# A state-space and expert layer split into two sequence halves that share one loop

## What is computed

```python
xn = layernorm(x)                                  # (4, 512, 128)
# branch 1: a diagonal state-space scan, 16 states per channel
dt = softplus(xn @ W_dt.T + b_dt)
state[n] = exp(-dt * exp(A_log[:, n])) * state[n] + dt * B[:, n] * xn      # along the sequence
y = sum_n state[n] * C[:, n] + D * xn
# branch 2: 64 experts (128 -> 32 -> 128), top 8 of a softmax router, and 2 shared experts (128 -> 256 -> 128)
cw = normalised top-8 of softmax(xn @ router_w + router_b)                 # (tokens, 64)
routed = sum_e cw[:, e] * (silu(xn @ W1[e] + b1[e]) @ W2[e] + b2[e])
shared = sum_s silu(xn @ SW1[s] + sb1[s]) @ SW2[s] + sb2[s]
x = x + y + routed + shared
```

## Time and profile before

| what | us |
|---|---|
| median of 3 runs | 466.41 (465.42 to 468.53) |
| span of the profiled execution | 473.9 |
| TensorE busy | 346.5 |
| VectorE busy | 347.8 |
| ScalarE busy | 261.5 |
| GpSimd busy | 243.2 |

### The profile page before, as it was taken

The page is one execution under the profiler, slowest core; times in us unless marked ns, Lnnn a source line. Parts: engine busy times, 40 slices in busy tenths (PEclk is TensorE's granted clock), DMA queues, the critical chain, the costliest instruction groups (busy, mean ns, idle before and its releaser), DMA issues.

```text
span 473.9 us, 5780 instructions
## 1 busy us (share of the span) xinstructions
PE 346.5 (73%) x1491; PEld 247.2 (52%) x1491; DVE 347.8 (73%) x615; ACT 261.5 (55%) x440; POOL 243.2 (51%) x254
## 2 busy tenths in 40 slices
PE   1846879667975987779506848977887887887883
PEld 0435659356854866668403524544554554554542
DVE  5679998897864866648169759908688688688674
ACT  1477654546458346374505675355856856856820
POOL 3475300704763676776800049005577877877850
PEclk9977675959997898998956975997999999999997
DMA  6374100100111112120160000004658658668574
GB/s 175 94 200 128 25 1 1 45 11 24 46 39 29 34 41 81 43 42 21 35 190 0 0 0 2 0 0 89 126 101 161 123 116 163 122 119 162 112 152 111
DMA packets 36213, 35.09 MB, mean 74 GB/s; under 512 B 12166, under 2 KB 30839, under 8 KB 36183
## 3 DMA queue, kind: packets, MB, share of 16 engines
q0 software_dynamic: 7104, 21.90, 22.7%
q1 hardware_dynamic: 29078, 12.84, 10.2%
HBM read 13.29 MB, written 4.65 MB: 38 GB/s over the span
## 4 chain that ended last, share of the span: by engine, by line
PE 35%; POOL 19%; DVE 19%; issue 13%; ACT 6%; DMA 3%; another core or an unknown queue 2%; DVEq 1%; SPq 0%; POOLq 0%; ACTq 0%
POOL state L568 10%; PE psum L1376 5%; POOL xn_tok L572 4%; PE psum L1349 4%; POOL g_hi L581 3%; PE psum L1365 3%; PE psum L1389 3%; PE psum L1443 3%; PE psum L292 3%; PE psum L293 2%; PE psum L294 2%; PE psum L1352 2%; PE psum L1355 2%; PE psum L1338 1%
## 5 line engine op out<-in xcount | busy, mean ns | idle before, releaser
L1212 DVE TENSOR_TENSOR_SCAN state<-dec,win_t 128x1024 f32<-128x1024 f32 x32 | 73.4, 2293 | 26.5 <-ACT dec L777 26.5
L568 POOL TENSOR_SCALAR state<-state,ssm_cb 128x1024 f32<-128x1024 f32 x32 | 49.7, 1553 | 48.0 <-DVE state L1212 45.0
L812 ACT ACTIVATE sil<-psum,vec_t 128x512 f32<-128x512 f32 x64 | 43.2, 687 | 48.3 <-PE psum L294 37.7
L509 POOL DMA_INDIRECT parts<-t_out,part x39 | 41.0, 1050 | 48.3 <-ACT t_out L726 41.9
L1498 PE MATMUL psum<-hid,g_w 128*128 128x512 f32 x128 | 62.1, 599 | 0.0
L1221 DVE TENSOR_TENSOR hid<-sil,psum 128x512 f32<-128x512 f32 x64 | 41.7, 676 | 12.9 <-ACT sil L812 10.9
L497 POOL DMA_INDIRECT x_tile<-normed,token x39 | 41.3, 1059 | 13.4 <-issue 10.7
L292 PE MATMUL psum<-xn_hi,g_hi 128*128 128x512 f32 x64 | 39.7, 620 | 11.3 <-ACT sil L812 11.3
L1094 DVE TENSOR_TENSOR t_hid<-t_sil,psum 128x352 f32<-128x352 f32 x39 | 20.3, 521 | 32.3 <-ACT t_sil L710 23.5
L717 ACT ACTIVATE t_hid_t<-psum 128x384 f32<-128x384 f32 x39 | 19.2, 492 | 38.9 <-PE psum L1365 25.3
L1376 PE MATMUL psum<-w_out,t_hid_t 128*128 x234 | 37.5, 300 | 2.2 <-ACT t_out L726 1.4
(11 more groups left out here) (308 smaller groups left out, 887.6 us busy)
## 6 DMA issues: line engine op xcount, KB each, us to landing
xn_tok<-state POOLq DMA_DIRECT2D x32, 512.0 KB, 4.5
e_raw<-in_L_ffn_w SPq DMA_DIRECT2D x16, 128.0 KB, 2.2
both<-parts SPq DMA_DIRECT2D x4, 512.0 KB, 5.6
e_raw<-in_L_ffn_w SPq DMA_DIRECT2D x8, 176.0 KB, 2.6
res<-in_L_attn_x SPq DMA_DIRECT2D x4, 256.0 KB, 3.8
normed<-rows SPq DMA_DIRECT2D x1, 1024.0 KB, 5.2
g_raw<-in_L_ffn_w SPq DMA_DIRECT2D x16, 64.0 KB, 2.3
g_w<-in_L_ffn_w SPq DMA_DIRECT2D x16, 64.0 KB, 2.2
```

Source lines behind the costliest of these rows:

```text
L509: pool.indirect_dma_start(out=parts, out_offset=bass.IndirectOffsetOnAxis(ap=part[:, n:n + 1], axis=0), in_=t_out[n % ORING][:, :], in_off ...
L568: own(pool.tensor_scalar(state[k][:, :], state[k][:, :], ssm_cb[:, i * GPI + k // 2:i * GPI + k // 2 + 1], 0.0, ALU.mult, ALU.add))
L812: act.activation(sil[:, c % 2, :], ps[c % 2][:, :], ACT.Silu, bias=vec_t[:, V_B1 + c // NBLK:V_B1 + c // NBLK + 1]).then_inc(h_silu, 1)
L1212: dve.tensor_tensor_scan(state[k][:, :], dec[n % DECS][:, at_half], win_t[:, at_half], 0.0, ALU.mult, ALU.add).then_inc(scanned, 1)
```

## The change

The four blocks become two parts: blocks 0 and 1, then blocks 2 and 3. Each part is scanned and run through all 16 groups in 4 turns (4 groups by 2 blocks, and 4 states, in each), so there are 8 turns with 8 units and 4 scans each, as before. The first part's head runs alone; the second part's head (logits, `W_dt` products, shared experts, ranking, softplus, token weights) is spread over the first part's turns, and the first part's tail over turns 4 and 5. All expert weights are loaded at once (four DMAs for `g_raw1`, ahead of the shared weights in SyncE's queue, one for `g_w2` behind `both`), and GpSimd splits them in one piece before the loop. The selectors are float32r, in two tensors. Decays and scans are of one state and one half of the tokens, with 6 decay buffers. There are 4 silu buffers and 8 gated ones. Each selector product stands one unit later, behind the next unit's first product, and second products follow six products behind. The accumulating DMAs alternate between `y_t` and a second sum `y_2`, which is added at the end. GpSimd normalises the eight late tiles. The scans no longer alternate with pairs of gatings: two come first in a turn, one after two gatings, one at the end.

The core of the diff:

```diff
+        DECS, HRING = 6, 8
+        dec = [later(f"dec_{j}", [P, NTOK // 2]) for j in range(DECS)]
+        SRING = 4
+        LAG = 6
+        UNITS_BESIDE = {(0, 0, 2): [("logit", 0, 2), ("logit", 0, 3)], (0, 0, 4): [("delta", 0, 2)],
+                        (0, 0, 5): [("delta", 0, 3)], (0, 1, 2): [("shared", 0, 2), ("shared", 1, 2)],
+                        (0, 2, 2): [("shared", 2, 2), ("shared", 3, 2)],
+                        (0, 3, 3): [("shared", 0, 3), ("shared", 1, 3)],
+                        (0, 3, 5): [("shared", 2, 3), ("shared", 3, 3)]}
@@ SyncE
             sp.wait_ge(fr_dve, max(FR_DVE.values()))
+            for n in range(4):
+                at_e = slice(n * E1 // 4, (n + 1) * E1 // 4)
+                sp.dma_start(g_raw1[:, at_e, :], rw1[at_e, :, :].rearrange("e d h -> d e h")).then_inc(g_in, 16)
             sp.dma_start(sw1_raw[:, :, :], sw1.rearrange("e d h -> d e h")).then_inc(late_in, 16)
@@ GpSimd
+            pool.wait_ge(g_in, 16 * 4)
+            pool.wait_ge(both_used, 1)
+            split(raw, g_hi[:, :, :].rearrange("p g h -> p (g h)"), g_lo[:, :, :].rearrange("p g h -> p (g h)"))
+            pool.nop().then_inc(g_split, 1)
+            pool.wait_ge(late_root, 1)
+            for t in range(HT, NT):
+                pool.tensor_scalar(xn_tok[:, t, :], res[:, t, :], mv[:, t, 0:1], nrm[:, 2, t:t + 1],
+                                   ALU.subtract, ALU.mult).then_inc(late_tok, 1)
...
+            def add_state(m):
+                pool.wait_ge(scanned, m + 1)
+                own(pool.tensor_scalar(state[k][:, :], state[k][:, :], ssm_cb[:, n:n + 1], 0.0, ALU.mult, ALU.add))
+                if n >= 2:
+                    pool.wait_ge(y_in[(m - 2) % 4], 16 * ((m - 2) // 4 + 1))
+                y = (y_t, y_2)[n % 2]
+                pool.dma_start(y[:, h * HTOK:(h + 1) * HTOK], state[k][:, :], accum_op=ALU.add).then_inc(y_in[k], 16)
...
+            for m in range(2 * NS):
+                add_state(m)
+                if m in range(GPT, GPT + 3):
+                    poly_step(POOL_POLY[1], m - GPT)
+                if m == 13:
+                    skip_term(1)
@@ ScalarE, after the first part's head
+            for h, i in TURN_LIST:
+                for s in range(GSTEPS):
+                    for what in units_at(h, i, s):
+                        leave(what)
...
+                if (h, i) == (0, 0):
+                    softplus_exp(2)
+                    softplus_exp(3)
+                if (h, i) == (0, 1):
+                    choice_exp(1)
+                if (h, i) == (0, TURNS - 1):
+                    act.wait_ge(win_ready, NBLK)
+                    for m in states_of(1, 0):
+                        decay(m)
+                elif i < TURNS - 1:
+                    for m in states_of(h, i + 1):
+                        decay(m)
+                if (h, i) == (0, 1):
+                    softplus_log(2)
+                    softplus_log(3)
@@ VectorE, the head's end and the loop
+            join(0)
+            join(1)
+            variance(0)
+            reverse_root(0)
+            for t in range(HT):
+                normalise(t)
+            join(2)
+            low_part(0)
+            low_part(1)
+            join(3)
+            variance(1)
+            reverse_root(1)
+            dve.nop().then_inc(late_root, 1)
+            rank(0)
+            combine(0)
+            poly(0)
+            split_cw(0)
+            split_cw(1)
+            softplus(0)
+            softplus(1)
+            low_part(2)
+            low_part(3)
+            for h, i in TURN_LIST:
+                m = h * NS + i * GPT
+                scan(m)
+                scan(m + 1)
+                if (h, i) == (0, 1):
+                    rank(1)
+                if (h, i) == (0, 2):
+                    combine(1)
+                    poly(2)
+                if (h, i) == (0, 3):
+                    split_cw(2)
+                    softplus(2)
+                for s in range(GSTEPS):
+                    if s == 2:
+                        scan(m + 2)
+                    if (h, i, s) == (0, 3, 3):
+                        split_cw(3)
+                    if (h, i, s) == (1, 1, 4):
+                        finish(0)
+                        finish(1)
+                    weigh(h, i, s)
+                if (h, i) == (0, 3):
+                    softplus(3)
+                scan(m + 3)
+                if (h, i) == (1, 0):
+                    sum_up(0)
+                    sum_up(1)
@@ TensorE
+            def select(e):
+                pe.wait_ge(cw_split, b + 1)
+                if e >= 2:
+                    pe.wait_ge(hid_done, e - 1)
+                pe.matmul(ps[2 + e % 2][:, :], selector, blk(cw_hl, b), start=True, stop=True).then_inc(cwx_made, 1)
...
+                    for what in units_at(h, i, s):
+                        enter(what)
+                        if what[0] == "expert":
+                            selects(NTH_EXPERT[what])
+                        if what[0] in ("shared", "expert"):
+                            second_products(NTH_PRODUCT[what] - LAG + 1)
+                last = units_at(h, i, GSTEPS - 1)[-1]
+                if at_turn + 1 < len(TURN_LIST):
+                    ahead = [units_at(*TURN_LIST[at_turn + 1], s)[-1] for s in range(2)]
+                    enter(ahead[0])
+                    selects(NTH_EXPERT[ahead[0]])
+                    enter(ahead[1])
+                    selects(NTH_EXPERT[ahead[1]])
+                selects(NTH_EXPERT[last] + 1)
+                second_products(NTH_PRODUCT[last] + 1)
+                if at_turn + 1 < len(TURN_LIST):
+                    selects(NTH_EXPERT[last] + 3)
```

More of the change, by code:

```diff
@@ L184, in program @@
         tile_e = sb("tile_e", [1, NTILE], mybir.dt.int32)
+        routed = over(base, nc.sbuf_base)
+        prob, rest1 = (routed(n, [P, NT // 2, E1]) for n in ("prob", "rest1"))
         base = here()
@@ L590, in _ @@
+            for c in range(3):
+                poly_step(POOL_POLY[0], c)
+            skip_term(0)
+            for m in range(2 * NS):
[4 more added lines that the diff above has]
+                    skip_term(1)
         @block.scalar
@@ L807, in silu @@
[L807 to L824 removed]
+                act.wait_ge(g_split, 1)
@@ new lines, in _ @@
+            act.activation(warm[:, 0:1], half_pi[:, :], ACT.Sqrt)
+            root(0)
+            leave(("turn", 0, 0))
+            leave(("turn", 0, 1))
+            leave(("logit", 0, 0))
+            leave(("logit", 0, 1))
+            root(1)
+            leave(("delta", 0, 0))
+            leave(("delta", 0, 1))
+            choice_exp(0)
+            for b in range(HB):
+                softplus_exp(b)
+            for b in range(HB):
+                softplus_log(b)
+            leave(("shared", 0, 0))
@@ L1108, in _, with tiles_of, join @@
             dve.wait_ge(back_dve, max(BK_DVE.values()))
-            for b in range(NBLK):
+            def tiles_of(h):
+                return slice(h * HT, (h + 1) * HT)
+            def join(b):
                 dve.wait_ge(both_in[b], 16)
@@ L1245, in _ @@
+            for b in range(HB, NBLK):
+                sum_up(b)
+            for b in range(HB, NBLK):
+                finish(b)
         @block.tensor
@@ L1409, in _, with bank_of, turn_in_tokens @@
                     attention(b)
-            turn_tiles(xn_tok, 0, 2 * NT)
             pe.wait_ge(weights_split, 2)
             pe.wait_ge(late_in, 16 * 8)
-            for b in range(NBLK):
+            pe.wait_ge(sel_ready, 1)
+            def bank_of(what):
+                u = NTH[what]
+                if u >= 2:
+                    pe.wait_ge(h_left, u - 1)
+                return ps[u % 2]
+            def turn_in_tokens(b):
+                bank = bank_of(("turn", 0, b))
+                for n in range(TPB):
+                    if b < HB:
+                        pe.wait_ge(tok_ready, 2 * NT + b * TPB + n + 1)
+                    else:
+                        pe.wait_ge(late_tok, (b - HB) * TPB + n + 1)
+                    ins = pe.transpose(bank[:, n * P:(n + 1) * P], xn_tok[:, b * TPB + n, :], ident[:, :])
+                ins.then_inc(h_made, 1)
@@ L1456, in second_biases, with enter @@
+            def enter(what):
+                kind, k, b = what
+                if kind == "logit":
+                    logit(b)
+                if kind == "delta":
+                    delta(b)
+                if kind == "shared":
+                    shared_in(k, b)
+                if kind == "expert":
+                    expert_in(k, b)
             def second_biases(b):
                 pe.wait_ge(cw_copied, b + 1)
-                pe.matmul(ps[4 + b][:, :], b2_sb[:, :], cw_b2[:, b % 2, :], start=False, stop=False,
+                if b == NBLK - 1:
+                    pe.wait_ge(cw_split, NBLK)
+                pe.matmul(ps[4 + b][:, :], b2_sb[:, :], cw_b2[:, b % 2, :], start=b == NBLK - 1, stop=False,
@@ L1515, in _, with second_product @@
```

(15 more changed lines are left out.)

623 lines of the change are left out of this document (305 added, 318 removed).

## The result

The changed kernel takes 473.78 us (median of 4 runs, 472.45 to 474.68) against 466.72 (median of 4, 465.42 to 468.53) in the same job: ratio 1.0143, 95% interval 1.0106 to 1.018. The forecast was 465.9, so the change is some 7 us slower where no change was forecast. The profiled execution of after took 474.68 us, its span is 472.9.

The account below looks back on a forecast made before the run. No engine bounds the whole kernel; in the loop VectorE waits for ScalarE. Head -33.4, loop +29.6, tail -0.7, layer one +0.4 and port +3.6 sum to -0.5 us: 465.9 us, range 454 to 478.

Parts of the forecast that it names:

- Head -33.4: Layer two before the loop: with two blocks ahead instead of four, first scan at 286.8 instead of 320.19, -33.4 us.
- Rival four: Head shortens by 28 us, not 33, as GpSimd's split, polynomial and late tiles share one queue: 471; chance 0.06.
- Plain turn 16.2, VectorE waiting for the selector: Loop turns without extras: 16.2 us instead of 17.7, VectorE waiting for TensorE's selector, not for ScalarE.
- Rival one: Loop: engines slide past each other better, turns near their busiest engine; 450.9 or 458 us; chance 0.33.
- The queues of the four long turns: Loop turns 0 to 3, carrying the second part's head: 21.3, 21.3, 25.2 and 29.1 us, sum 96.9.
- Small packets: Layer one: expert weights as 8192 packets of 128 bytes ahead of shared weights cost 0; selector building there +0.4 us.
- rival three: Layer one: small packets come late, GpSimd waits at its 28th tile, about 5 us slip: 471; chance 0.08.
- Tail -0.7: After the last scan: two blocks instead of four, but two additions each: -0.7 us of 16.0.
- The port step: Loop, SBUF port shared by VectorE and GpSimd: one scan a turn loses 0.6 us in six turns, +3.6 us.
- the bounds of 0 to 16.8: Limits of the shared-port cost: 0 if the next scan keeps the port, 16.8 us if two scans a turn lose 1.05.
- Rival two: Loop: the shared port decides, two scans a turn lose 1.05 us each, polynomial and softplus 2 more: 481; chance 0.19.
- The signs named in the forecast: Wrong if plain turns are near 14.5, first four turns sum under 85 or over 105, or the tile loop ends later.

Follow-up runs that it names:

- experiment 6: Changed kernel with each selector product put back right behind its own unit's first product: 477.6 us, ratio 1.0205.
- the first profile: Profile of the kernel before that the forecast used, span 473.9 us; the second is from an unchanged repeat: 467.69 us, span 466.0.
- experiment 2: Changed kernel without GpSimd's multiplications of the states by B times C: 464.35 us, ratio 0.993.
- experiment 10: Changed kernel, three scans still in a row, with ranking, polynomial, softplus and a weight split moved behind gatings in turns 1 to 3: 463.82 us, ratio 0.9928.
- experiment 3: Changed kernel with a VectorE scan after every second gating instead of three in a row: 455.56 us, ratio 0.975.

## Why the prediction was wrong

Right:
- *Head -33.4.* Measured -33.5, first scan 46.7 us behind the first sum (45.6 by the forecast's 241.20 and 286.8). The closeness is in part luck: against the first profile's 79.0 us it is -32.3, and the head of before was 1.2 us longer in the second. Rival four falls.
- *Plain turn 16.2, VectorE waiting for the selector.* 16.4, with that wait. Rival one (tighter turns) falls for plain turns. Having the selector late does not cause the wait: with it at once a plain turn takes 18.0 us (experiment 6).
- *The queues of the four long turns.* 96.9 forecast, 97.2 in experiment 2, where the port is silent. Single turns are off by up to 1.6 us (25.2 against 23.6, 29.1 against 30.4) and cancel, so the closeness of the sum is in part luck.
- *Small packets.* The first sum starts at 234.6 instead of 233.3. The forecast had +0.4; not the 5 us of rival three.
- *Tail -0.7.* -1.9, a small miss to the good side.

Wrong: the step "I take one scan a turn by 0.6 ... in the six turns in which no silu hides it: +3.6 us". The port step was the one that failed: its size, its place and its mechanism fall.
- Size: 10.2 us in the loop (177.5 against 167.3), and none in the kernel before (136.7 against 136.5). That lies inside the bounds of 0 to 16.8. Rival two (the port decides, slower) is nearest to what happened, with 473.8 instead of its 481, but not by its mechanism: it had two scans delayed in every turn, and in the plain turns none is.
- Place: nothing in turns 5 to 7, where the forecast had half of it; 9.4 in turns 2 and 3, in the steps of the second part's head. The forecast's rival two named these as "polynomial and softplus meet multiplications too" and gave them 2 us.
- Mechanism: the forecast had one scan a turn lose 0.6 us. In after, five of the seven GpSimd instructions that were issued during a scan with another directly behind it waited through both, and no scan lost anything. The rule that issue order decides who blocks (the Trainium skill, SBUF — State Buffer, Who interferes with whom), by which the forecast read the trace, is not borne out there: the multiplication was issued at 426.82, before the third scan, which lost nothing. It is borne out in turn 2, by the other two, where the scans behind took 3.31 and 3.13 us. How long after the start of the scan the multiplication comes does not tell the cases apart: 0.18 us after it, one took 5.11 us in the plain turn of after, and in turn 2 of experiment 10 one took 3.00 and the next scan 3.13. What decides is open. Single scans lose too (3.73 and 2.92 us in turns 0 and 1), but those turns grow by 0.1 and 0.7 us only. The rest of the direct loss falls on the second part's own steps: 2.48 instead of 0.73 us for a predicated copy, 2.25 instead of 0.69 for the next one (1.45 in experiment 2), 1.53 instead of 0.67 for a product. The exclusion itself, which the same section states, fits every one of these waits.
- What made 3.5 and 2.5 us of VectorE's delay into 5.2 and 4.2: TensorE's work that needs no gating runs out. In turn 3 the six held-back second products (5.31 us), and the first products behind them, are done at 363.76, 11.9 us after the three scans began, and the first gating comes at 365.57. The forecast counted the held-back products as cover and not what happens when they run out: an idle of 2.6 to 3.4 us and, behind it, products at half clock. It priced VectorE's delay one to one.

The signs named in the forecast were met as it said: the four first turns sum to 107.4 us, over the 105 beyond which it was to be wrong.

The second slip is the base. The terms are differences, so layer one's extra 8 us in the profile did not enter their sum. The first turn of before did: 17.3 us in the first profile and 16.3 in the second, most of the 1.2 us between the loop's 137.7 and 136.5. Of the 7.4 us between forecast and profile, the port step is 6.6 and this 1.2; the first sum (0.9) and the tail (-1.2) nearly cancel. Layer one's 8 us made the two spans look equal (473.9, 472.9), and whoever compares only those finds no change at all.

What remains: moved steps or alternating scans take back 10 and 18 us. Alternating is the larger one because it shortens turn 1 (20.8 against 22.5 with moved steps), turn 2 (23.4 against 25.2) and turn 5 (14.7 against 16.4) further. That alternating without the port still beats experiment 2 by 9 us of loop (158.1 against 167.3) is shown. That the cause is TensorE's stock of work lasting over a shorter stretch without gatings is argued from turn 3 and experiment 10. It fits turn 2, where the stretch is 15.8 us in after, 12.3 in experiment 2 and 10.7 in experiment 3, and TensorE's wait for a gating 3.44, 0.44 and 0.77 us; in turn 5 it was not tested apart.

## What to carry to other kernels

When work is fitted into a loop, count for every engine how long it goes without feeding the next one, and set that beside the stock (buffers, held-back products) that bridges it. In turns 2 and 3 a stretch longer than the stock cost its excess, and at TensorE the clock on top. Put such steps between the loop's own feeding steps and not in one piece at the turn's head: moving four of them, with nothing else changed, gave 10 us here (the ranking alone, in turn 1, gave nothing that the turn shows). And take the profile of the kernel before twice, if the change is expected to be small beside what one execution may differ in another stage.

## What the hardware showed that was not expected

- Three scans back to back on VectorE can shut GpSimd out for two whole scans: 5.11 us for a multiplication that takes 1.11 alone, while the three take 6.65 us. They do not always: in turn 2 the three took 8.56 us.
- A multiplication of GpSimd costs VectorE up to 1.75 us in one instruction (a predicated copy, 2.48 against 0.73).
- TensorE came back at half clock after 3.44 us idle in turn 2. In turn 3 it came back at full clock after 2.65 us and again after 1.90, and fell to half 1.6 us later (granted 0.50 from 372.3 to 375.5); after 1.91 us alone (experiment 2, turn 3) it kept full clock, with products at 0.39 to 0.40 us. The same idle of 3.25 us in turn 5 was followed by half clock in after and by full clock in experiment 10, and the turns took 17.4 and 16.4 us.
- The end of layer one differed by 8 us between two executions of the same kernel (first sum at 241.2 and 233.3). The profiles of the other kernels have it at 233.7 to 235.8.
